# A decoder layer's feed-forward: gate and up by seven half-size products, their result through memory, then down in five slabs

## The chip, the cores and the metric

The kernel is one program on 1 core of a Trainium2 chip. The metric is the time of one execution on the device, in microseconds (us). TensorE, VectorE, ScalarE and GpSimd compute, SyncE issues the transfers; in the rows they are PE (PEld for its weight loads), DVE, ACT, POOL and SP.

## The reference

`x` has 4 sequences of 512 rows of 1024 numbers, 2048 rows in all, in float32. Self-attention and cross-attention come first and are not touched. What is changed is the last line:

```python
x = x + ffn(layernorm(x))
# Wg, Wu: 3584 x 1024, Wd: 1024 x 3584, each from 4-bit codes:
#   w = NF4_CODE[q];  w = w.reshape(-1, 64) * absmax[:, None]
g = x @ Wg.T
u = x @ Wu.T
h = silu(g) * u
y = h @ Wd.T
```

## The kernel before, in words

`attention` runs first and leaves its result `x2` in memory. `feed_forward` is a block of its own, each engine with its instruction list, joined by counting semaphores. An engine takes its list in order: a wait holds all that stands behind it.

**Numbers.** A float32 value `v` is cut into a float16 high part `v_h` (ScalarE) and the rest `v_l = v - v_h` (GpSimd, for the inputs VectorE), and a product is three matmuls: h·h, h·l, l·h.

**Weights.** The 3584 hidden columns are 28 chunks of 128. A chunk has a gate, an up and a down matrix of 128 x 1024, each made in two *tiles* of 128x512. For a tile SyncE loads `codes` (L1380) and `scales` (L1385), two tiles ahead. ScalarE draws eight straight lines of the codes (`draw_line`, L1547 and L1550), VectorE joins them by six maxima (L1625) and one difference (L1631), GpSimd multiplies by the scales (`scale`, L1426), ScalarE cuts the high part (L1555) and GpSimd the low (L1431). ScalarE's table of lines mixes the tiles: the high part of tile k is cut between lines of tile k+2.

**Input.** Sixteen rows of 128 of `x2` are kept in float32 in `y` (L1396). Each is normalised (statistics at L1639 to L1644, root on GpSimd at L1436, ScalarE at L1561), turned by TensorE (L1483) and cut (L1569, L1652), in part between the first matmuls.

**Products.** A group is two chunks; there are 14 groups. `gate_up` (L1501) makes for a chunk and a sequence the 128x512 gate and up, 24 matmuls each; ScalarE takes silu (L1578), VectorE multiplies (L1661), the result is cut into `hT_h` and `hT_l` (L1583, L1445). `down` (L1521) then makes for each of the 16 rows of 128 the group's share of the output, 12 matmuls, and VectorE adds it to `y` (L1666). So a group is 384 + 192 matmuls of 128x512, and the whole 14 x 576 = 8064. The group is a loop over one body, but for the first and the last. `out` is stored behind the last group's adds (L1404).

## Time and profile before

| | |
|---|---|
| median of 3 runs | 2796.19 us (2792.77 to 2798.71) |
| the profiled execution | 2796.21 us, its span 2794.3 us |
| busy: TensorE, VectorE, ScalarE, GpSimd | 92%, 74%, 56%, 44% of the span |
| feed-forward's first instruction | 950.7 us from the span's start |
| TensorE's share of the chain of waits | 60% (L1501 39%, L1521 21%) |

A matmul's recorded time overlaps with the next one's, so the pace is read from how many a stretch holds. A wait is put down to what came last.

### The profile page before, as it was taken

To read this page: it belongs to the slowest core of one execution; us is meant where nothing else is said; L and a number is where in the kernel's file an instruction comes from. 1 tells how busy PE (TensorE), PEld (TensorE's weight loads), DVE (VectorE), ACT (ScalarE), POOL (GpSimd) and SP (SyncE) were. 2 spreads that over 40 slices of the span, in tenths; PEclk is the share of its full clock that TensorE was granted. 3 is DMA by queue.
4 is the path that set the end of the run, shared out by engine and by line. 5 is a ranking of instruction groups with operands and counts; after the bars stand their busy time and mean duration, and the time that the engine had idled before them with its cause. 6 is when DMAs were issued, how large, how long until landed. Compare 5 with 4: busy or idle time off the path is not lost.

```text
span 2794.3 us, 52658 instructions
## 1 busy us (share of the span) xinstructions
PE 2581.9 (92%) x18536; PEld 1397.0 (50%) x18536; DVE 2054.9 (74%) x2844; ACT 1572.4 (56%) x2794; POOL 1235.5 (44%) x1068
## 2 busy tenths in 40 slices
PE   5889999999974359899999999999999999999999
PEld 3567767667663234344444444444444444444444
DVE  4656768767775768787787869788787868778773
ACT  3456666656663468474655647465564747465550
POOL 2356667767774424252433424243433425243330
PEclk9999999999987669999999999999999999999999
DMA  5243433333222321111111112121111212111112
GB/s 192 91 132 100 121 114 120 102 111 100 81 73 59 128 80 56 51 61 38 60 49 50 53 45 60 38 68 38 53 52 45 61 38 66 40 60 46 52 34 120
DMA packets 153268, 205.34 MB, mean 73 GB/s; under 512 B 34160, under 2 KB 85872, under 8 KB 153072
## 3 DMA queue, kind: packets, MB, share of 16 engines
q1 hardware_dynamic: 153072, 202.97, 23.0%
q8 instruction: 93, 1.52, 0.2%
q14 instruction: 103, 0.84, 0.1%
HBM read 157.16 MB, written 44.04 MB: 72 GB/s over the span
## 4 chain that ended last, share of the span: by engine, by line
PE 60%; DVE 2%; issue 1%; ACT 1%; DMA 1%; POOL 0%; SPq 0%; DVEq 0%; ACTq 0%; POOLq 0%
PE f_bank L1501 39%; PE f_down L1521 21%; DVE line L1625 1%; DMA codes<-in_codes 1%; DVE f_stats L1639 0%; DVE fT_l L1652 0%; ACT f_xn L1561 0%; ACT line L1550 0%; ACT fT_h L1569 0%; PE f_down L1483 0%; DVE w L1631 0%; ACT line L1547 0%; DVE h L1661 0%; DVE y L1666 0%; DVE f_mean_var L1642 0%
## 5 line engine op out<-in xcount | busy, mean ns | idle before, releaser
L1625 DVE TENSOR_TENSOR line<-line 128x512 f32<-128x512 f32 x1008 | 919.4, 962 | 46.7 <-issue 30.9
L1550 ACT ACTIVATE line<-codes 128x512 f32<-128x512 int32 x1008 | 591.2, 620 | 382.6 <-DVE line L1625 284.8
L1501 PE MATMUL f_bank<-fT_h,up_h 128*128 128x512 f16 x1792 | 680.2, 380 | 3.7 <-DVE fT_l L1652 2.4
L1501 PE MATMUL f_bank<-fT_l,up_h 128*128 128x512 f16 x1792 | 680.2, 380 | 0.0
L1501 PE MATMUL f_bank<-fT_h,up_l 128*128 128x512 f16 x1792 | 680.2, 380 | 0.0
L532 POOL TENSOR_TENSOR p_l<-p,p_h 128x512 f16<-128x512 f32 x320 | 369.9, 1164 | 243.0 <-ACT p_h L945 242.6
L1666 DVE SCALAR_TENSOR_TENSOR y<-f_down,y 128x1024 f32<-128x1024 f32 x224 | 274.2, 1224 | 190.7 <-PE f_down L1521 190.7
L1431 POOL TENSOR_TENSOR up_l<-w,up_h 128x512 f16<-128x512 f32 x112 | 145.8, 1301 | 529.2 <-ACT up_h L1555 529.2
L1426 POOL TENSOR_TENSOR w<-w,scales 128x512 f32<-128x512 f32 x168 | 263.8, 1570 | 227.7 <-DVE w L1631 227.7
L1115 DVE TENSOR_REDUCE block_max<-bank 128x4 f32<-128x512 f32 x320 | 218.8, 686 | 195.3 <-PE bank L704 193.0
L1521 PE MATMUL f_down<-dn_h,hT_h 128*128 128x512 f16 x896 | 340.6, 380 | 9.0 <-DVE y L1666 9.0
L937 ACT ACTIVATE p<-bank 128x512 f32<-128x512 f32 x320 | 190.9, 597 | 271.6 <-PE bank L733 269.7
L1521 PE MATMUL f_down<-dn_l,hT_h 128*128 128x512 f16 x896 | 340.6, 380 | 0.0
L1521 PE MATMUL f_down<-dn_h,hT_l 128*128 128x512 f16 x896 | 340.4, 380 | 0.0
L1501 PEld LDWEIGHTS f_bank<-fT_h,up_h 128*128 128x128 f16 x1792 | 175.5, 98 | 214.7 <-DVE fT_l L1652 2.8
L1501 PEld LDWEIGHTS f_bank<-fT_h,up_l 128*128 128x128 f16 x1792 | 175.5, 98 | 212.1 <-issue 1.1
L1501 PEld LDWEIGHTS f_bank<-fT_l,up_h 128*128 128x128 f16 x1792 | 175.5, 98 | 210.3 <-issue 0.6
L1445 POOL TENSOR_TENSOR hT_l<-h,hT_h 128x512 f16<-128x512 f32 x112 | 172.9, 1543 | 237.3 <-ACT hT_h L1583 237.3
L1547 ACT ACTIVATE line<-codes,above 128x512 f32<-128x512 int32 x168 | 119.9, 714 | 218.3 <-DVE line L1625 183.6
L674 PE MATMUL bank<-xT,w_h 128*128 128x512 f16 x720 | 220.2, 388 | 10.8 <-POOL vx_h L602 10.8
L1661 DVE SCALAR_TENSOR_TENSOR h<-f_bank,h 128x512 f32<-128x512 f32 x112 | 77.1, 688 | 164.5 <-PE f_bank L1501 156.6
L945 ACT ACTIVATE p_h<-p 128x512 f16<-128x512 f32 x320 | 192.0, 621 | 0.0
(157 smaller groups left out, 4245.4 us busy)
## 6 DMA issues: line engine op xcount, KB each, us to landing
codes<-in_codes SPq DMA_DIRECT2D x168, 256.0 KB, 3.0
scales<-in_scales SPq DMA_DIRECT2D x336, 128.0 KB, 2.9
nat_parts<-nat SPq DMA_DIRECT2D x48, 256.0 KB, 2.0
q_rows<-nat_parts SPq DMA_DIRECT2D x96, 128.0 KB, 2.7
x_unit<-in_x SPq DMA_DIRECT2D x64, 128.0 KB, 2.7
x<-x_unit SPq DMA_DIRECT2D x64, 128.0 KB, 2.3
y<-x SPq DMA_DIRECT2D x4, 2048.0 KB, 12.3
out<-y SPq DMA_DIRECT2D x16, 512.0 KB, 2.6
```

The lines of the kernel that those rows point to most:

```text
L532: nc.gpsimd.tensor_tensor(p_l[:, n % 2, k, :], p32[:, f % 3, :], p_h[:, n % 2, k, :], ALU.subtract).then_inc(p_low, 1)
L674: mm = nc.tensor.matmul(dst[:, :], w[:, c, cols], xT[:, :, half, c, :], start=(c == 0 and m == 0), stop=(c == CT - 1 and m == 2))
L937: nc.scalar.activation(p32[:, f % 3, :], bank[T_BANK + T_OF[f % CHUNKS]][:, :], ACT.Exp, scale=SELF_SCALE).then_inc(t_exp, 1)
L945: nc.scalar.activation(p_h[:, n % 2, k, :], p32[:, f % 3, :], ACT.Copy).then_inc(p_high, 1)
L1115: nc.vector.reduce_max(block_max[:, n % PAIRS, k, :], bank[S_BANK + S_OF[k]][:, :].rearrange("p (a n) -> p a n", n=P), AX_X)\
L1426: nc.gpsimd.tensor_tensor(w, w, scales[:, k % 2, :], ALU.mult).then_inc(scaled, 1)
L1445: nc.gpsimd.tensor_tensor(hT_l[:, q // NB, cols], h32[:, q % 2, :], hT_h[:, q // NB, cols], ALU.subtract).then_inc(h_low, 1)
L1501: mm = nc.tensor.matmul(bank[(GATE, UP)[kind] + n % 2][:, :], w[:, chunk, kind, P * c:P * c + P], x[:, c, cols], start=(m == 0), stop=(m = ...
L1521: mm = nc.tensor.matmul(down_bank[r % 2][:, half, :], h[:, m // 3, rows], w[:, m // 3, cols], start=(m == 0), stop=(m == 5))
L1550: op = nc.scalar.activation(line[:, m, :], codes[:, slot, :], ACT.Copy, scale=slope, bias=intercept)
L1625: nc.vector.tensor_tensor(line[:, n + 2, :], line[:, n, :], line[:, n + 2, :], ALU.max)\
L1666: nc.vector.scalar_tensor_tensor(y[:, r, :], down_bank[r % 2][:, :, :].rearrange("p a n -> p (a n)"), 1.0 / (H_SCALE * F_SCALE), y[:, r, : ...
```

## The change

`feed_forward` is written anew; nothing else is touched. 

**Phase 1, gate and up.** Take one matrix product for two chunks (256 columns), all 1024 inputs and two sequences; cut in halves along each side it is 2 x 2 blocks times 2 x 2 blocks. Instead of eight half-size products it makes seven, M1 to M7, of sums and differences of the blocks (Strassen's scheme), 12 matmuls each. The sums of the inputs are made once: the rows are taken in 8 *pairs* (row j and j + 8), turned, summed (`sums`), and kept as seven float16 pairs in `fx`. The sums of the weights are made per `k` (k even: gate of two chunks, odd: up; 28 values of k), from four *quarters* (tiles): GpSimd sums (`sum_w`), ScalarE and GpSimd cut, into one of two sides of `fw`. A *set* is the seven products for one k and one of two row halves (`nb`): 56 sets of 84 matmuls, 4704 in all. M4, M5 and M7 go on top of M2, M3 and M1 in PSUM, after ScalarE has copied M2 and M1 away and VectorE has taken a difference (`differ`); `join`, `left`, `right_sum` and `right` put the four result blocks together. Beside each set, in `half_step`, every engine makes two tiles of the next weights. The hidden values are stored to memory (`store_h`), 256 KB for each of 112 blocks.

**Tiles.** The six maxima are replaced by two `reduce_max`, each over four lines of 512 (2048 inputs, 512 outputs; the four numbers that it compares lie 2 KB apart).

**Phase 2, down.** `y` is loaded again, into space that the inputs had. The 28 chunks are five slabs of 3, 4, 7, 7 and 7. For each slab and each row of 128 the hidden values come back from memory (seven slots), 6 matmuls per chunk follow, and one add to `y`: 80 adds in place of 224. The tiles of a slab are made during the slab before, the first slab's in the last two half steps of phase 1 (three tiles in each). A row takes 18, 24 or 42 matmuls; phase 2 has 2688, as before.

The loop is gone: all is written out.

```diff
-y = sb("y", [P, RT, C], FP32)
-xT_h = sb("fT_h", [P, CT, B * T], FP16)
-xT_l = sb("fT_l", [P, CT, B * T], FP16)
+fx = sb("fx", [P, 2, 7, 2, KT * HALF], FP16)
+fw = sb("fw", [P, 2, 7, 2, HALF], FP16)
...
+PRODUCTS = (M2, M1, M3, M6, M4, M5, M7)
+POS = {m: n for n, m in enumerate(PRODUCTS)}
+PS_OF = {M1: 0, M2: 1, M3: 2, M6: 3, M4: 1, M5: 2, M7: 0}
+
+CUT = (M2, M4, M1, M3, M6, M5, M7)
+SUMMED = (M2, M1, M6, M5, M7)
+DIRECT = {M4: 1, M3: 2}
...
+SLABS = (3, 4, 7, 7, 7)
...
+    def store_h(n):
+        chunk, b, _ = h_at(n)
+        sp.wait_ge(h_low, n + 1)
+        sp.dma_start(dram["h"][QT * b:QT * b + QT, :, chunk, :].rearrange("q p n -> p q n"),
+                     h_box[:, n % BOXES, :, :, :].rearrange("p q a n -> p q (a n)"))\
+            .then_inc(box_stored[n % BOXES], 16)
...
+    for idx in range(3):
+        load_h(idx)
+    for h in range(8 * GROUPS - 4, 8 * GROUPS):
+        store_h(h)
+    sp.wait_ge(product, 7 * NSET)
+    for r in range(4):
+        sp.dma_start(y_row(r), dram["x2"][r // QT, P * (r % QT):P * (r % QT) + P, :]).then_inc(y_loaded[r], 16)
+    for idx in range(3, H_SLOTS):
+        load_h(idx)
+    sp.wait_ge(h_low, 8 * GROUPS)
+    for r in range(4, RT):
+        sp.dma_start(y_row(r), dram["x2"][r // QT, P * (r % QT):P * (r % QT) + P, :]).then_inc(y_loaded[r], 16)
+    for idx in range(NI):
+        for t in tiles_in(idx):
+            if t + 2 < LAST_TILE:
+                load_tile(t + 2)
+        if idx >= NI - RT:
+            r = idx - NI + RT
+            sp.wait_ge(y_added, idx + 1)
+            sp.dma_start(dram["out"][P * r:P * r + P, :], y_row(r)).then_inc(out_stored, 16)
+        if H_SLOTS <= idx + H_SLOTS - 1 < NI and idx >= 1:
+            load_h(idx + H_SLOTS - 1)
+    sp.wait_ge(out_stored, 16 * RT)
...
+    def pair(j):
+        for n in range(4):
+            x_cut_low(j, n)
+        if j + 2 < 8:
+            root(j + 2)
+        for n in range(4, 7):
+            x_cut_low(j, n)
...
+    def half_step(k, nb):
+        s = 2 * k + nb
+        tiles = tiles_of(k, nb)
+        last = s - 1
+        lows = [h_tile(last // 4, last % 2, c) for c in H_ORDER] if last >= 0 and last // 2 % 2 else []
+        for n in lows[0:2]:
+            hidden_low(n)
+        if nb == 1 and k + 1 < NK:
+            cut_low(k + 1, M2)
+            cut_low(k + 1, M4)
+        scale(tiles[0])
+        if nb == 0 and k >= 0:
+            cut_low(k, M5)
+            cut_low(k, M7)
+        if nb == 1 and k + 1 < NK:
+            sum_w(k + 1, M1)
+        if k >= 0:
+            join(s)
+        if nb == 1 and k + 1 < NK:
+            sum_w(k + 1, M6)
+        for n in lows[2:4]:
+            hidden_low(n)
+        if nb == 1 and k + 1 < NK:
+            cut_low(k + 1, M1)
+            cut_low(k + 1, M3)
+        scale(tiles[1])
+        if nb == 0 and k + 1 < NK:
+            sum_w(k + 1, M2)
+        if nb == 1 and k + 1 < NK:
+            sum_w(k + 1, M5)
+            cut_low(k + 1, M6)
+            sum_w(k + 1, M7)
...
-    def gate_up(i, chunk, first=False):
-        for nb in range(NB):
-            n = NB * chunk + nb
-            cols = slice(T * nb, T * nb + T)
-            if first:
-                pe.wait_ge(ln_low, 8 * (nb + 1))
-            for kind in range(2):
-                if nb == 0:
-                    pe.wait_ge(w_low, PER * i + 4 * chunk + 2 * kind + 2)
-                if n >= 2:
-                    pe.wait_ge((silu_done, h_done)[kind], NQ * i + n - 1)
-                for m in range(3 * CT):
-                    c = m // 3
-                    w, x = ((up_h, xT_h), (up_h, xT_l), (up_l, xT_h))[m % 3]
-                    mm = nc.tensor.matmul(bank[(GATE, UP)[kind] + n % 2][:, :],
-                                          w[:, chunk, kind, P * c:P * c + P], x[:, c, cols],
-                                          start=(m == 0), stop=(m == 3 * CT - 1))
-                    if m == 3 * CT - 1:
-                        mm.then_inc((gate_done, up_done)[kind], 1)
-                    if first and nb < NB - 1 and kind == 0 and m % 6 == 5:
-                        ln_turn(4 * (nb + 1) + m // 6)
+    def multiply(s, m):
+        k, nb = s // 2, s % 2
+        pe.wait_ge(w_low, 7 * k + CUT_AT[m] + 1)
+        if m == M4:
+            pe.wait_ge(copied, 2 * s + 1)
+        if m == M5:
+            pe.wait_ge(differed, s + 1)
+        if m == M7:
+            pe.wait_ge(copied, 2 * s + 2)
+        out = ps[:, 4 * (s % 2) + PS_OF[m], :]
+        for n in range(3 * KT):
+            c = n // 3
+            w, x = ((0, 0), (0, 1), (1, 0))[n % 3]
+            mm = nc.tensor.matmul(out, fw[:, k % 2, m, w, P * c:P * c + P],
+                                  fx[:, nb, m, x, HALF * c:HALF * c + HALF],
+                                  start=(n == 0 and m in (M1, M2, M3, M6)),
+                                  stop=(n == 3 * KT - 1), skip_group_check=m in (M4, M5, M7))
+        mm.then_inc(product, 1)
+
+    def product_set(s):
+        if s < 2:
+            pe.wait_ge(x_low, 28 * (s + 1))
+        else:
+            pe.wait_ge(right_done, s - 1)
+        for n, m in enumerate(PRODUCTS):
+            multiply(s, m)
+            if s == 0 and n in (0, 1, 3):
+                turn((5, 6, None, 7)[n])
...
+    def half_step(k, nb):
+        s = 2 * k + nb
+        tiles = tiles_of(k, nb)
+        last = s - 1
+        highs = [h_tile(last // 4, last % 2, c) for c in H_ORDER] if last >= 0 and last // 2 % 2 else []
+        draw(tiles[0], 0)
+        if k >= 0:
+            copy(s, 0)
+        if last >= 0 and last // 2 % 2 == 0:
+            silu(last, C22)
+            silu(last, C11)
+        for n in highs[0:2]:
+            hidden_high(n)
+        if nb == 1 and k + 1 < NK:
+            cut_high(k + 1, M2)
+            cut_high(k + 1, M4)
+        draw(tiles[0], 1)
+        if k >= 0:
+            copy(s, 1)
+        for n in highs[2:4]:
+            hidden_high(n)
+        if nb == 0 and k >= 0:
+            cut_high(k, M5)
+            cut_high(k, M7)
+        draw(tiles[1], 0)
+        if nb == 1 and k + 1 < NK:
+            cut_high(k + 1, M1)
+            cut_high(k + 1, M3)
+        draw(tiles[1], 1)
+        if nb == 1 and k + 1 < NK:
+            cut_high(k + 1, M6)
...
+    for idx in range(NI):
+        for t in tiles_in(idx):
+            draw(t, 0)
+            draw(t, 1)
+            down_high(t)
...
-    def look_up(i, ops):
-        for at in ops:
-            k, n = at // LUT, at % LUT
-            t = AHEAD + PER * i + k
-            if n < LUT - 1:
-                dve.wait_ge(lined, NL * t + n + 3)
-                if n >= 2:
-                    dve.wait_ge(lut, LUT * t + n - 1)
-                nc.vector.tensor_tensor(line[:, n + 2, :], line[:, n, :], line[:, n + 2, :], ALU.max)\
-                    .then_inc(lut, 1)
-            else:
-                dve.wait_ge(lut, LUT * t + n)
-                if k >= 2 - AHEAD:
-                    dve.wait_ge(w_low, t - 1)
-                nc.vector.tensor_tensor(w32[:, k % 2, :], line[:, NL - 2, :], line[:, NL - 1, :], ALU.subtract)\
-                    .then_inc(lut, 1)
+    def reduce(t, which):
+        dve.wait_ge(lined, 8 * t + 4 * which + 4)
+        if t >= 1:
+            dve.wait_ge(lut, LUT * t)
+        nc.vector.reduce_max(side[:, which, :], line[:, which, :, :].rearrange("p m n -> p n m"), AX_X)\
+            .then_inc(lut, 1)
...
+    def half_step(k, nb):
+        s = 2 * k + nb
+        up = k % 2
+        tiles = tiles_of(k, nb)
+        if s >= 1:
+            finish(s - 1)
+        look_up(tiles[0])
+        if k >= 0:
+            differ(s)
+        reduce(tiles[1], 0)
+        if k >= 0:
+            left(s)
+            if up:
+                dve.wait_ge(left_done, s + 1)
+                times_gate(s, C22, c32[:, 0, :])
+        reduce(tiles[1], 1)
+        subtract(tiles[1])
+        if k + 1 == NK:
+            look_up(tiles[2])
+        if k >= 0:
+            for n, c in enumerate((C21, C12)):
+                if up:
+                    dve.wait_ge(product, 7 * s + POS[(M4, M5)[n]] + 1)
+                    times_gate(s, c, bank(s, 1 + n))
+                right_sum(s, n)
...
+    for j in range(8):
+        sums(j)
+        if j + 2 < 8:
+            stat(j + 2)
+            normal(j + 2)
+        if j == 0:
+            half_step(-1, 0)
+        if j == 2:
+            half_step(-1, 1)
+    for k in range(NK):
+        for nb in range(2):
+            half_step(k, nb)
+    finish(NSET - 1)
+    for idx in range(NI):
+        for t in tiles_in(idx):
+            look_up(t)
+        add_down(idx)
```

ScalarE in the last group before: lines (L1547, L1550), `h` from the banks (L1578) and high cuts (L1555) are mixed.

```order
L1547 ACTIVATE line<-codes,above 128x512 [waits lut,codes_loaded0]
L1547 ACTIVATE line<-codes,below 128x512 [waits lut]
L1550 ACTIVATE line<-codes 128x512 [waits lut]
L1555 ACTIVATE up_h<-w 128x512 [waits scaled]
L1550 ACTIVATE line<-codes 128x512 [waits lut]
L1583 ACTIVATE hT_h<-h 128x512 [waits h_done]
L1550 ACTIVATE line<-codes 128x512 [waits lut] x4
L1547 ACTIVATE line<-codes,above 128x512 [waits lut,codes_loaded1]
```

And ScalarE in phase 2 of the change (`fx` is where the down weights lie there, L1765 is `down_high`, L1738 and L1741 are `draw`):

```order
L1738 ACTIVATE line<-codes,above 128x512 [waits lut,codes_loaded1]
L1741 ACTIVATE line<-codes 128x512 x3
L1738 ACTIVATE line<-codes,below 128x512 [waits lut]
L1741 ACTIVATE line<-codes 128x512 x3
L1765 ACTIVATE fx<-quarter 128x512 [waits product,scaled]
L1738 ACTIVATE line<-codes,above 128x512 [waits lut,codes_loaded0]
```

The high cut of a tile now stands between its own lines and the next tile's, and waits for that tile's scaling.

GpSimd at the half step of even k and nb = 0 (L1582 `hidden_low`, L1553 `scale`, L1569 `cut_low` of M5 and M7, L1588 `join`):

```order
L1582 TENSOR_TENSOR h_box<-h,h_box 128x4x128 [waits h_high] x2
L1553 TENSOR_TENSOR quarter<-quarter,scales 128x512 [waits lut,scales_loaded0]
L1569 TENSOR_TENSOR fw<-w_sum,fw 128x512 [waits fw_high] x2
L1588 TENSOR_TENSOR c<-c 128x512 [waits differed,copied]
L1582 TENSOR_TENSOR h_box<-h,h_box 128x4x128 [waits h_high] x2
L1553 TENSOR_TENSOR quarter<-quarter,scales 128x512 [waits lut,scales_loaded1]
```

`scale` of the next chunk's first tile, which needs both of its reduces, stands ahead of the low cuts of M5 and M7, which TensorE waits for in the same set.

## Rows read from the trace of the kernel before

**Rows 1.** The page: busy us (share of the span) x instructions, by engine
```profile
PE 2581.9 (92%) x18536; PEld 1397.0 (50%) x18536; DVE 2054.9 (74%) x2844; ACT 1572.4 (56%) x2794; POOL 1235.5 (44%) x1068
```
**Rows 2.** The chain of waits in order of time: start us, us, what
```profile
1173.85 82.88 PE f_bank L1501 x384
...
2748.57 41.45 PE f_down L1521 x192
2790.05 1.23 DVE y L1666
```
**Rows 3.** Windows: us, busy (x) of PE, PEld, DVE, ACT, POOL, clock, DMA share, GB/s
```profile
1346.00:2600.00 1254.00, 1254.00 (x5812) 568.49 (x5811) 991.68 (x1090) 715.81 (x1254) 474.41 (x325) 1.00 0.16 51
955.40:1050.00 94.60, 42.92 (x197) 25.05 (x198) 67.97 (x124) 62.07 (x106) 27.31 (x54) 0.66 0.35 122
969.50:990.00 20.50, 0.00 (x0) 0.00 (x0) 15.05 (x25) 6.88 (x14) 5.88 (x4) 0.50 0.99 366
```
**Rows 4.** Groups by line: xcount | busy us, mean ns | idle before
```profile
L1625 DVE TENSOR_TENSOR line<-line 128x512 f32<-128x512 f32 x1008 | 919.4, 962 | 46.7 <-issue 30.9 <-ACT line L1550 11.5 <-ACT line L1547 4.3
L1666 DVE SCALAR_TENSOR_TENSOR y<-f_down,y 128x1024 f32<-128x1024 f32 x224 | 274.2, 1224 | 190.7 <-PE f_down L1521 190.7
L1115 DVE TENSOR_REDUCE block_max<-bank 128x4 f32<-128x512 f32 x320 | 218.8, 686 | 195.3 <-PE bank L704 193.0
L1067 DVE TENSOR_SCALAR xn<-xn,mean_var,rstd 128x1024 f32<-128x1024 f32 x14 | 11.3, 806 | 1.6 <-POOL rstd L526 1.6
L1661 DVE SCALAR_TENSOR_TENSOR h<-f_bank,h 128x512 f32<-128x512 f32 x112 | 77.1, 688 | 164.5 <-PE f_bank L1501 156.6 <-ACT h L1578 7.1
```
**Rows 5.** Timeline, ScalarE at one tile: start us, us, instruction [idle before]
```profile
989.89 0.72 ACT L1547 ACTIVATE line<-codes,above 128x512 f32<-128x512 int32 x1 [13.62 <-DMA codes<-in_codes]
990.52 0.70 ACT L1547 ACTIVATE line<-codes,below 128x512 f32<-128x512 int32 x1
991.13 3.21 ACT L1550 ACTIVATE line<-codes 128x512 f32<-128x512 int32 x6
994.25 0.61 ACT L1555 ACTIVATE up_h<-w 128x512 f16<-128x512 f32 x1
```
**Rows 6.** Timeline, ScalarE's passes back to back in the steady part
```profile
1701.14 0.58 ACT L1578 ACTIVATE h<-f_bank 128x512 f32<-128x512 f32 x1
1701.62 0.62 ACT L1550 ACTIVATE line<-codes 128x512 f32<-128x512 int32 x1
```
**Rows 7.** GpSimd by line: duration ns min/median/max, first and last start
```profile
L1426 POOL TENSOR_TENSOR w<-w,scales x168: 1257/1711/1724, 960.6 to 2713.8; 128x512 f32<-128x512 f32 x168
...
L1431 POOL TENSOR_TENSOR up_l<-w,up_h x112: 1151/1314/1622, 963.6 to 2686.5; 128x512 f16<-128x512 f32 x112
```
**Rows 8.** Timeline, hand-over from VectorE to GpSimd
```profile
966.14 0.69 DVE L1631 TENSOR_TENSOR w<-line 128x512 f32<-128x512 f32 x1
...
967.01 1.26 POOL L1426 TENSOR_TENSOR w<-w,scales 128x512 f32<-128x512 f32 x1 [2.06 <-DVE w L1631]
```
**Rows 9.** Timeline, the pieces of a layernorm row
```profile
979.86 1.28 DVE L1639 BATCH_NORM_STATS2 f_stats<-y 128x6 f32<-128x512 f32 x2
981.18 0.21 DVE L1642 BATCH_NORM_AGGREGATE f_mean_var<-f_stats 128x2 f32<-128x12 f32 x1
...
996.14 0.55 POOL L1436 TENSOR_TENSOR f_rstd<-f_var_eps,f_minus_half 128x1 f32<-128x1 f32 x1
...
998.11 1.94 PE L1483 MATMUL f_down<-f_ident,f_xn 128*128 128x128 f32 x8 [52.06 <-ACT f_xn L1561]
```
**Rows 10.** Timeline, SyncE's issues at the start and of y
```profile
950.94 0.34 SPq L1380 DMA_DIRECT2D codes<-in_codes  x1
...
969.52 1.68 SPq L1396 DMA_DIRECT2D y<-x  x3
...
971.31 3.26 SPq L1380 DMA_DIRECT2D codes<-in_codes  x1
```

763 lines of the change are left out of this document (464 added, 299 removed).

## The prediction

> **What bounds the kernel now.** I read the page first: TensorE is busy 92% of the span, VectorE 74% [rows 1]. A mean over stages says little, so next the chain of waits: from 1173.85 us on it is TensorE alone, 384 matmuls in 82.88 us and 192 in 41.45 us, up to one last add [rows 2]. That is 0.2158 us per matmul, no gap, and the clock of that stretch is 1.00, TensorE's upper level of 2.4 GHz [rows 3]. Feed-forward's 8064 matmuls at that pace are 1740.3 us. They end at 2790.0, so TensorE works as if it had started at 1049.7 without a stop; the block's first load is issued at 950.94 [rows 10], so its start costs 98.8 us. VectorE is busy 992 of 1254 us in the steady part, ScalarE 716 [rows 3]: they are hidden, with 21% and 43% to spare.
>
> **What is taken away.** 5376 gate and up matmuls become 4704: 672 x 0.2158 = **145.0 us**. Down keeps 2688, 580.1 us. A set of 84 takes 18.13 us, a product of 12 takes 2.59. All else is whether the other engines still hide.
>
> **Prices.** ScalarE: the eight lines of a tile take 4.45 us, so one side of four 2.25 [rows 5]; other passes follow each other at 0.48 to 0.55, I take 0.5 [rows 6]. VectorE: a pass of 512 is 0.69 long and one of 1024 is 1.22 [rows 4], so 0.54 per 512 numbers and 0.15 fixed, and two stand 0.60 apart [rows 9]. GpSimd: 1.26 for scaling and 1.15 for a cut at the shortest [rows 7], and 0.18 from VectorE's end to its start [rows 8]. For the new `reduce_max` of 2048 numbers there is no row. Its nearest is the reduce of 512 at 0.686, whose numbers lie side by side [rows 4]. At the same rate it is 4 x 0.536 + 0.15 = 2.30 us; at the upper end, with two steps for each number since they lie 2 KB apart, 4.44. I take 2.30, as no strided operation in these rows is seen to be slower.
>
> **The start, +33.** A pair of rows needs on GpSimd seven low cuts and a root (8.6 us), but not in one piece. The root of pair j+2 stands in the middle of pair j and waits for statistics that VectorE takes only behind pair j's five sums. There are three slots for sums, so the fourth waits for the third low cut. By the pieces of rows 9: about 4.7 us to the last sum, 3.3 for the statistics of two rows, 0.75 for the root, three cuts 3.5, so 12.5 to 13 us a pair for six pairs and 8.7 for two. The normalising pass is 0.81 per row [rows 4] and lies beside the cuts. The first pair begins some 16 us in. Two half steps of tiles lie between (10 and 14 us). The first set starts some 93 us after the first load, and three turns of 3.9 us (16 transposes, [rows 9]) lie between its products. It then stops at M4: that waits for ScalarE's copy, which waits for all eight pairs' cuts, at about 138. M5 waits until 144.5, the second set starts at 149.7. Less one set, this is a start at 131.6 in place of 98.8. Bounds: 10 if the roots don't hold GpSimd, 45 if the engines hinder each other.
>
> **Phase 1, +62.** In four sets (72.5 us) VectorE has 16 reduces, 8 subtractions, 20 passes on the banks and 8 products: 58 us. ScalarE has some 55, GpSimd 51. None is full, but each list is in order and the chain goes round all three. From the start of a second set of odd k (0): M2 is done at 2.8, ScalarE copies, cuts two results and two weights, draws the lower side of tile 1 (7.65); reduce and subtraction (10.7), scaling and one sum (13.2), cuts of M1 and M3 (14.3), the lower side of tile 2 (16.6), reduce and subtraction (19.9), two products and two sums (22.3), the last block and its product (24.0), the next set's copy and two cuts (25.6), lower side (27.9), reduce and subtraction (30.9), scaling (32.4), and only then the low cut of M5 (33.5). TensorE wants it at 18.1 + 5 x 2.59 = 31.1: 2.4 us late. Walked on, the fourth set's last product comes 2.4 us after the point at which this round began with its copy, so the round itself is that much longer: 4.8 us per four sets, 13 rounds, 62 us. Bounds: 14 with one microsecond a round, 91 with seven.
>
> VectorE's maxima take 0.96 in the mean and its plain passes on a bank 0.69 [rows 4], and GpSimd's scaling 1.71 in the median against 1.26 at the shortest [rows 7]: here the two hinder each other. By the Trainium skill (SBUF — State Buffer, section "SBUF: two separate sides") a VectorE operation with two SBUF inputs and a GpSimd one exclude each other, and a reduce with one input would not; then the shortest times are right, and with the medians instead the sum would be some 17 us longer.
>
> **Phase 2, +82.** The last two half steps make three tiles each, with high cuts that wait for scalings: by the same walk row 0 ends 11 us late. Then 9.2 MB of `y` and hidden values are asked for before the codes of the ninth tile. Before, 7.5 MB went in 20.5 us [rows 3], and ScalarE stood 13.6 us for codes that were issued behind three loads of `y` [rows 5, 10]. So those codes come about 25 us after the loads, and they start only when the last hidden values are cut, 17 us after the nominal end of phase 1.
>
> From there a loop binds. ScalarE's list is draw, draw, high cut, and the cut waits for the tile's own scaling. A tile takes 4.45 + 0.05 + 2.30 + 0.72 + 0.18 + 1.26 + 0.1 + 0.5 = **9.6 us**. Slab 1 has 16 rows x 24 x 0.2158 = 82.9 us of matmuls and must see 14 tiles: 134 us. Slab 0 (62.2 us) ends with its sixth tile after the codes, at 43 + 58 = 101 us. In slabs 2 and 3 a row is 9.06 us and 14 tiles fit into 16 rows (134 against 145). They and slab 4 go at TensorE's pace, 3 x 145.0 less 7.8 of their first row that is done while it waits: 427. Together 101 + 134 + 427 = 662 against 580. VectorE's adds (80 in place of 224, at 1.22) lie in the gaps. Bounds: 60 to 100.
>
> **Sum.** -145.0 + 33 + 62 + 82 = +32. The sum stands against the profiled execution's 2796.2 us, which is the median (2796.19) too: **2828 us**.
>
> **The rivals.**
> *The lists of phase 1 run far enough apart* (faster). If the low cut of M5 and the copy of the next round come before TensorE wants them, phase 1 costs nothing: -145 + 33 + 82 = -30, 2766 us. It decides at 2.4 us in a chain of 33, so at 7% of it: ScalarE's spare 43% and hand-overs shorter than I count speak for it, the medians in rows 7 against.
>
> *Each number of the strided reduce costs two steps* (far slower). At 4.44 us VectorE has 16 x 4.36 + 23 = 93 us in four sets against 72.5: +281 over 14 rounds. A tile in phase 2 takes 2.25 + 8.9 + 2.7 = 13.9: 43 + 48 tiles x 13.9 + 145 - 8 = 847, +267. The start takes 17 more. -145 + 33 + 281 + 17 + 267: about 3250 us. Rows 4 show a reduce at full rate, but on numbers side by side, so they neither bear it out nor exclude it. The Trainium skill (Advanced Engine Details and Errata, "SBUF Cachelines") says that a 16-byte line wants two hits to hide its latency, and here each access is on another line; no row of before shows that penalty.
>
> *The change gives less than its 672 matmuls*, if the products on top of others don't go back to back. The matmuls have the same shape and the same two operands' places as before, so I give it nothing of its own.
>
> **Chances.** The forecast (three places bind, 2787 to 2900) has 0.50; the fast rival 0.30, from 2725 with a cheap start to 2785; the strided reduce 0.17; 0.03 is left for an end above 2925 for other reasons or below 2725. The range is 2725 to 2925; it leaves out the strided reduce and that rest. Of the forecast case 0.01 is faster and 0.05 within 0.2%, which is about what a measurement of this kernel can tell from no change. So faster 0.31, same 0.05, slower 0.64. The likeliest case's own range is 2787 to 2900.
>
> **What would show it.** In the profile after: 4704 + 2688 matmuls of 512 columns; TensorE's idle time before M5 on GpSimd's low cut, some 5 us in every four sets; in slabs 0 and 1 TensorE waiting for down weights at 9.6 us per tile, and none in slabs 2 to 4; ScalarE's idle time before its high cut, 4.4 us per tile; the reduce at 2.3 us. A reduce near 4.4 makes the forecast wrong by hundreds; phase 1 in 1015 us makes it wrong by 62; a first set not held at M4 by 20 or more.

## The result: 3178.6 us, and the profile after

The changed kernel takes **3178.55 us** (median of 4 runs, 3176.19 to 3182.88) against 2795.79 before (4 runs on the same chip): ratio 1.1371, interval 1.1354 to 1.1388. The forecast was 2828, its range 2725 to 2925; the rival that priced the strided reduce at two steps per number had about 3250. The profiled execution took 3180.82 us, its span is 3179.0.

The page of the changed kernel: busy us by engine, and the shares of the chain that ended last.
```profile
PE 2564.3 (81%) x17864; PEld 1356.6 (43%) x17864; DVE 2427.2 (76%) x2332; ACT 1635.4 (51%) x2998; POOL 1519.0 (48%) x1363
...
DVE 18%; PE 16%; issue 9%; ACT 8%; POOL 5%; DMA 1%; SPq 0%; DVEq 0%; POOLq 0%; ACTq 0%
```
The 672 matmuls are gone (18536 [rows 1] to 17864), and still the kernel is 383 us longer. The chain of before was TensorE alone from 1173.85 us on [rows 2]; now VectorE, ScalarE and GpSimd hold more of it than TensorE. VectorE has 512 instructions fewer than before and is busy for 372 us more. Its groups, and the two others that matter (xcount | busy us, mean ns of one | idle before, ended by):
```profile
L1916 DVE TENSOR_REDUCE side<-line 128x512 f32<-128x2048 f32 x336 | 1247.7, 3727 | 209.4 <-ACT line L1741 208.8
L1682 PE MATMUL f_ps<-fx,fw 128*128 128x512 f16 x4704 | 1103.4, 398 | 197.1 <-POOL fw L1569 152.1
...
L1553 POOL TENSOR_TENSOR quarter<-quarter,scales 128x512 f32<-128x512 f32 x168 | 213.6, 1272 | 968.5 <-DVE quarter L1928 968.5
```
One reduce takes 3.73 us, not 2.30. The work that it replaces, three maxima of 0.96 [rows 4], took 2.9. The 4704 matmuls of phase 1 are all there.

The trace by stage: sets 2 to 56 of phase 1 (from the 85th of its 4704 matmuls on), then phase 2 (length, busy us and instructions of PE, PEld, DVE, ACT, POOL, granted clock, DMA share, GB/s).
```profile
1130.20:2386.40 1256.20, 1076.91 (x4621) 461.84 (x4619) 1151.14 (x716) 761.61 (x1410) 726.06 (x601) 0.93 0.23 70
2386.40:3174.70 788.30, 620.23 (x2688) 269.99 (x2688) 503.48 (x240) 254.38 (x460) 132.12 (x109) 0.89 0.29 93
```
In the steady part of before, TensorE had no gap at a clock of 1.00 and VectorE was busy 79% of the time [rows 3]. In phase 1 now VectorE is busy 92%, TensorE stands idle for 179 us, and its 4620 matmuls take 80 us more than 0.2158 each. So a stop costs twice, once as idle time and once in the clock behind it.

One round of four sets in phase 1, TensorE's timeline (start us, us, instruction, [idle before]):
```profile
1668.17 34.06 PE L1682 MATMUL f_ps<-fx,fw 128*128 128x512 f16 x144 [6.09 <-POOL fw L1569]
1702.92 5.35 PE L1682 MATMUL f_ps<-fx,fw 128*128 128x512 f16 x24 [0.68 <-POOL fw L1569]
1712.13 19.63 PE L1682 MATMUL f_ps<-fx,fw 128*128 128x512 f16 x84 [3.86 <-POOL fw L1569]
1734.36 19.98 PE L1682 MATMUL f_ps<-fx,fw 128*128 128x512 f16 x84 [2.60 <-DVE c L1936]
1759.70 30.53 PE L1682 MATMUL f_ps<-fx,fw 128*128 128x512 f16 x133 [5.37 <-POOL fw L1569]
```
The round is 91.5 us in place of 72.5: 12.5 of idle time (0.68, 3.86, 2.60, 5.37) and 6.5 of slower matmuls. The mean of the 13 rounds is 90.9.

One tile of phase 2, ScalarE, VectorE and GpSimd:
```profile
2611.77 0.71 ACT L1738 ACTIVATE line<-codes,below 128x512 f32<-128x512 int32 x1
2611.89 7.25 DVE L1916 TENSOR_REDUCE side<-line 128x512 f32<-128x2048 f32 x2 [3.15 <-ACT line L1741]
...
2619.18 0.69 DVE L1928 TENSOR_TENSOR quarter<-side 128x512 f32<-128x512 f32 x1
...
2620.02 1.26 POOL L1553 TENSOR_TENSOR quarter<-quarter,scales 128x512 f32<-128x512 f32 x1 [9.09 <-DVE quarter L1928]
...
2621.31 0.63 ACT L1765 ACTIVATE fx<-quarter 128x512 f16<-128x512 f32 x1 [7.28 <-POOL quarter L1553]
...
2621.85 0.70 ACT L1738 ACTIVATE line<-codes,above 128x512 f32<-128x512 int32 x1
```
This is the loop that the prediction walked: draw, draw, reduce, subtract, scale, high cut, draw. Its period is 12.3 us, not 9.6. With a reduce of 2.30 the first one hides behind the drawing of the lower side, with 3.73 both lie on the path (7.25 in one piece). Fourteen tiles at 12.3 are 172 us, so now slabs 2 and 3 are bound too: TensorE's last waits for a slab's weights end at 2684.5, 2859.9 and 3035.3, 175 us apart in place of 145. Only what follows goes at TensorE's pace.

Where the miss lies, by stage. The right column is experiment e_pairs, in which the reduce takes 2.28 us:

| us | forecast | changed kernel | reduce at 2.28 |
|---|---|---|---|
| second set starts at | 1100.6 | 1130.2 | 1114.6 |
| sets 2 to 56 | 1059.0 | 1256.2 | 1109.8 |
| phase 2 | 662.0 | 788.3 | 670.9 |

The forecast's column is its own sum: 950.94 + 149.7, then 55 sets at TensorE's pace (997.0) + 62, then 580 + 82. The columns differ by 30 + 197 + 126 = 353 us (the whole miss), and by 14 + 51 + 9 = 74 where the reduce has its forecast price.

### The profile page after: what moved, and what is told of

It reads as the page before. It is cut to its first block, busy times and chain, and to the rows that moved or that the text cites. A ratio compares the mean times of both kernels' runs of the same rounds, so it can differ in the third digit from the quotient of the medians.

```text
span 3179.0 us, 47439 instructions
## 1 busy us (share of the span) xinstructions
PE 2564.3 (81%) x17864; PEld 1356.6 (43%) x17864; DVE 2427.2 (76%) x2332; ACT 1635.4 (51%) x2998; POOL 1519.0 (48%) x1363
## 4 chain that ended last, share of the span: by engine, by line
DVE 18%; PE 16%; issue 9%; ACT 8%; POOL 5%; DMA 1%; SPq 0%; DVEq 0%; POOLq 0%; ACTq 0%
DVE side L1916 13%; PE f_ps L1682 11%; PE f_ps L1714 5%; ACT line L1741 4%; POOL quarter L1553 3%; DVE quarter L1928 2%; ACT line L1738 2%; POOL fw L1569 1%; DVE h L1942 1%; DVE c L1972 1%; ACT h_box L1813 1%; ACT fw L1753 1%; DMA codes<-in_codes 1%; DVE c L1961 0%; POOL c L1588 0%
## 5 line engine op out<-in xcount | busy, mean ns | idle before, releaser
L1916 DVE TENSOR_REDUCE side<-line 128x512 f32<-128x2048 f32 x336 | 1247.7, 3727 | 209.4 <-ACT line L1741 208.8
L1682 PE MATMUL f_ps<-fx,fw 128*128 128x512 f16 x4704 | 1103.4, 398 | 197.1 <-POOL fw L1569 152.1
L1682 PEld LDWEIGHTS f_ps<-fx,fw 128*128 128x128 f16 x4704 | 471.7, 102 | 827.4 <-POOL fw L1569 183.0
L1553 POOL TENSOR_TENSOR quarter<-quarter,scales 128x512 f32<-128x512 f32 x168 | 213.6, 1272 | 968.5 <-DVE quarter L1928 968.5
L1741 ACT ACTIVATE line<-codes 128x512 f32<-128x512 int32 x1008 | 556.0, 615 | 0.0
L1714 PE MATMUL f_ps<-fx,fw 128*128 128x512 f16 x1188 | 279.3, 398 | 84.1 <-POOL fx L1576 54.5
L1714 PE MATMUL f_ps<-fx 128*128 128x512 f16 x924 | 211.2, 390 | 52.6 <-POOL fx L1576 43.3
L1714 PEld LDWEIGHTS f_ps<-fx,fw 128*128 128x128 f16 x1188 | 119.9, 102 | 241.1 <-POOL fx L1576 57.6
L1765 ACT ACTIVATE fx<-quarter 128x512 f16<-128x512 f32 x44 | 27.7, 630 | 333.5 <-POOL quarter L1553 333.5
L1561 POOL TENSOR_TENSOR w_sum<-quarter 128x512 f32<-128x512 f32 x140 | 181.8, 1299 | 10.6
L1569 POOL TENSOR_TENSOR fw<-w_sum,fw 128x512 f16<-128x512 f32 x140 | 161.1, 1159 | 31.7 <-ACT fw L1753 31.7
L697 PE MATMUL bank<-k_rows,q_rows 96*128 96x512 f16 (+3 forms) x512 | 136.8, 306 | 18.7 <-DMA q_rows<-nat_parts 12.3
L1582 POOL TENSOR_TENSOR h_box<-h,h_box 128x512 f16<-128x512 f32 x112 | 134.1, 1217 | 36.4 <-ACT h_box L1813 35.8
L726 PE MATMUL bank<-q_rows,k_rows 97*128 97x512 f16 (+3 forms) x512 | 136.6, 305 | 14.5 <-DVE px_l L1149 10.4
```

Of the source, the lines that this page charges most:

```text
L1553: nc.gpsimd.tensor_tensor(w, w, scales[:, t % 2, :], ALU.mult).then_inc(scaled, 1)
L1561: nc.gpsimd.tensor_tensor(w_sum[:, SUM_SLOT[m], :], quarter[:, a, :], quarter[:, b, :], op)\
L1569: nc.gpsimd.tensor_tensor(fw[:, k % 2, m, 1, :], w_source(m), fw[:, k % 2, m, 0, :], ALU.subtract)\
L1682: mm = nc.tensor.matmul(out, fw[:, k % 2, m, w, P * c:P * c + P], fx[:, nb, m, x, HALF * c:HALF * c + HALF], start=(n == 0 and m in (M1, M ...
L1714: mm = nc.tensor.matmul(ps[:, 2 * (idx % 4) + half, :], hT[:, n, h, :], d[:, w, HALF * half:HALF * half + HALF], start=(n == 0 and m == 0) ...
L1741: op = nc.scalar.activation(out, codes[:, t % 2, :], ACT.Copy, scale=slope, bias=intercept)
```

## The experiments

Each kernel starts from the changed one, and each ratio is to the kernel before on the same chip; over the chips used the kernel before takes 2795.6 to 2798.0 us, so a difference between two experiments on different chips is good to some 2 us. The edits are shown without their semaphores. Two theories stand first. **A**: the reduce is slow since the four numbers of each output lie 2 KB apart. **B**: it is slow since each output takes only four numbers (short runs), or the loops around VectorE would stop TensorE at any price of it.

### a_maxima: three maxima in place of the reduce

```diff
-nc.vector.reduce_max(side[:, which, :], line[:, which, :, :].rearrange("p m n -> p n m"), AX_X)
+for m in (0, 2):
+    nc.vector.tensor_tensor(line[:, which, m, :], line[:, which, m, :], line[:, which, m + 1, :], ALU.max)
+nc.vector.tensor_tensor(side[:, which, :], line[:, which, 0, :], line[:, which, 2, :], ALU.max)
```


> Of the changed kernel, only the price of a side is changed: three maxima of 512 in place of the reduce over four lines that lie 2 KB apart (3.73 us in its profile). Theory 1, the reduce is the step that was mis-sized and the rest of the forecast's sum holds: a side costs 1.9 to 2.3 us (three passes 0.6 to 0.72 apart), the tile loop of phase 2 falls from 12.3 to 9.3 to 9.6 us, the round of four sets of phase 1 from 91.3 to 74 to 80 us, and the time is 2800 to 2870. Theory 2, the loops round the engines are what costs and the reduce only lies in them: rounds stay above 85 us and the time above 2950. If the maxima and GpSimd hinder each other as before the change (0.96 a maximum), the rounds lie at 80 to 84 and the time at 2860 to 2930.

Measured: 3018.14 us, ratio 1.0793 (1.0775 to 1.0811), 160 us less than with the reduce. Groups of VectorE and GpSimd in this kernel:
```profile
L1918 DVE TENSOR_TENSOR line<-line 128x512 f32<-128x512 f32 x672 | 677.5, 1048 | 174.6 <-ACT line L1742 172.6
L1921 DVE TENSOR_TENSOR side<-line 128x512 f32<-128x512 f32 x336 | 323.3, 962 | 11.6
```
```profile
L1570 POOL TENSOR_TENSOR fw<-w_sum,fw 128x512 f16<-128x512 f32 x140 | 192.5, 1383 | 25.5 <-ACT fw L1754 25.5
...
L1589 POOL TENSOR_TENSOR c<-c 128x512 f32<-128x512 f32 x56 | 96.0, 1714 | 0.0
```
A side takes 2.98 us (1001 us over 336), so it is cheaper than the reduce of 3.73. In the changed kernel the same two GpSimd operations take 1.16 and 1.27. Beside maxima GpSimd grows slower, beside reduces it does not: what VectorE gains here GpSimd gives back in part, and the round in phase 1 is 89.3 us, hardly shorter. In a round VectorE's busy time falls only from 83.2 to 79.5 us and GpSimd's rises from 53.2 to 62.8. No run shows by itself that GpSimd's rise is what keeps the round long. Phase 2 gains: a tile takes 9.2 us, and the last three slabs run as one stretch of 429.07 us (forecast 427). Time and round are those of theory 2 in the expectation, but a side came out at 2.98 us and not at 1.9 to 2.3, so this run doesn't yet tell the price from the loops.

### b_side_by_side: the four numbers next to each other

```diff
-line = sb("line", [P, 2, 4, HALF], FP32)
+line = sb("line", [P, 2, HALF, 4], FP32)
...
-out = line[:, which, m, :]
+out = line[:, which, :, m]
...
-nc.vector.reduce_max(side[:, which, :], line[:, which, :, :].rearrange("p m n -> p n m"), AX_X)
+nc.vector.reduce_max(side[:, which, :], line[:, which, :, :], AX_X)
```


> The lines are laid out so that the four numbers that a reduce compares lie side by side; ScalarE writes each line at every fourth place. Theory 1 (the distance of the reads costs): the reduce falls to 2.3 us and the time to 2800 to 2880, if ScalarE's writes cost no more. Rival (each output of only four inputs costs an extra, whatever the place): the reduce stays at 3.7 and the time at 3178. If ScalarE's writes 16 bytes apart become slow in their turn, its passes are over 0.62 and the gain is in part gone.

Measured: 3191.71 us, ratio 1.1419 (1.1399 to 1.1439). Groups of VectorE and of ScalarE:
```profile
L1916 DVE TENSOR_REDUCE side<-line 128x512 f32<-128x2048 f32 x336 | 767.3, 2284 | 687.7 <-ACT line L1741 687.5
```
```profile
L1741 ACT ACTIVATE line<-codes 128x512 f32<-128x512 int32 x1008 | 1008.5, 1144 | 0.0
```
The reduce of the same 2048 numbers falls to 2.28 us, the forecast's own price, with runs as short as ever: theory A. But ScalarE now writes at a distance of 16 B and takes 1.14 per line where it took 0.615, so the penalty has moved to the writer. It costs as much there, since ScalarE stands in both loops. It is the last case of the expectation, with nothing left of the gain.

### c_draw_ahead: ScalarE draws the next tile before it waits

```diff
-for idx in range(NI):
-    for t in tiles_in(idx):
-        draw(t, 0)
-        draw(t, 1)
-        down_high(t)
+late = [t for idx in range(NI) for t in tiles_in(idx)]
+for n, t in enumerate(late):
+    draw(t, 0)
+    draw(t, 1)
+    if n >= 1:
+        down_high(late[n - 1])
+down_high(late[-1])
```


> Only ScalarE's order in phase 2 is changed: it draws tile t+1 before it cuts the high part of tile t; the reduce is left. Theory (a serial loop draw, reduce, scale, cut of 12.3 us per tile binds phase 2): the period falls to what VectorE needs, two reduces, a subtraction and its adds, 9 to 9.5 us, and slabs 2 and 3 come to TensorE's 145 us: 100 to 120 us less, 3060 to 3080. Rival (VectorE or the transfers are the bound of phase 2 anyway): less than 30 us.

Measured: 3067.37 us, ratio 1.0969 (1.0950 to 1.0988), 111 us less, with the reduce as slow as before. ScalarE in phase 2:
```profile
2804.32 0.72 ACT L1738 ACTIVATE line<-codes,above 128x512 f32<-128x512 int32 x1 [2.75 <-DVE side L1918]
...
2810.10 0.61 ACT L1765 ACTIVATE fx<-quarter 128x512 f16<-128x512 f32 x1
2813.46 0.72 ACT L1738 ACTIVATE line<-codes,above 128x512 f32<-128x512 int32 x1 [2.75 <-DVE side L1918]
```
The high cut waits for a scaling 3 times (23 us), where it waited 52 times (396 us), and the period is 9.14 us, set by VectorE, which is busy for 9.11 of it. So phase 2 was bound by the order of one list, as forecast. The reduce's price entered through it, and in part through VectorE itself: with this order phase 2 takes 678 us here and 616 with the reduce at 2.28 (g_pairs_draw_ahead).

### d_probes: the price by distance

At the end of the changed kernel, behind its last use of `line`, VectorE makes single operations on it, twice over, and ScalarE writes copies into it.
```diff
+for b in (1, 2, 4, 8, 16, 128, 512):
+    tick(nc.vector.reduce_max(side[:, 0, :].rearrange("p (a b) -> p a b", b=b),
+                              flat(0).rearrange("p (a m b) -> p a b m", m=4, b=b), AX_X))
+tick(nc.vector.reduce_max(side[:, 0, 0:32], flat(0).rearrange("p (n m) -> p n m", m=64), AX_X))
+tick(nc.vector.reduce_max(side[:, 0, 0:32], flat(0).rearrange("p (m n) -> p n m", n=32), AX_X))
...
```


> The changed kernel with a row of single operations behind its end, each waiting for the one before; some 60 to 70 us longer. On VectorE the same reduce of 2048 float32 numbers to 512 with its four inputs 4, 8, 16, 32, 64, 512 and 2048 bytes apart, and to 32 outputs of 64 inputs each, near and far; a maximum of two 512-number operands in line and at distances of 1 KB, 512 B, 256 B and 16 B; on ScalarE a copy written in line and at every fourth place. Theory 1: the time follows the distance (2.3 us at 4 and 8 bytes, 3.7 from 16 bytes on, also with 64 inputs per output). Rival: 3.7 at every distance with four inputs, 2.3 with 64 inputs.

Measured (one execution, 3245.92 us). VectorE's timeline, four numbers per output at 4, 8, 16, 32, 64, 512 and 2048 B from each other, then 64 numbers per output at 4 B and at 128 B:
```profile
3174.64 2.29 DVE L2070 TENSOR_REDUCE side<-line 128x512 f32<-128x2048 f32 x1 [2.84 <-ACT line L1885]
3176.96 2.29 DVE L2070 TENSOR_REDUCE side<-line 128x512 f32<-128x2048 f32 x1
3179.28 3.77 DVE L2070 TENSOR_REDUCE side<-line 128x512 f32<-128x2048 f32 x1
3183.09 3.78 DVE L2070 TENSOR_REDUCE side<-line 128x512 f32<-128x2048 f32 x1
3186.91 3.57 DVE L2070 TENSOR_REDUCE side<-line 128x512 f32<-128x2048 f32 x1
...
3194.16 3.62 DVE L2070 TENSOR_REDUCE side<-line 128x512 f32<-128x2048 f32 x1
3197.82 2.29 DVE L2072 TENSOR_REDUCE side<-line 128x32 f32<-128x2048 f32 x1
3200.14 3.57 DVE L2073 TENSOR_REDUCE side<-line 128x32 f32<-128x2048 f32 x1
```
The step lies between 8 and 16 B, and beyond it distance changes little. With 64 numbers per output the two prices are the same 2.29 and 3.57: short runs cost nothing, and B's first half falls. Two-input maxima of 512 are dearer too once operands and output are out of line (0.69 in line, 1.07 to 1.25 at 16 to 1024 B; nothing between was tried), and so are ScalarE's copies (0.63 in line, about 1.1 written at every fourth place).

### e_pairs: pairs of neighbours

A layout with 8 B between the numbers of an output, and in which ScalarE writes two neighbours at a time:
```diff
-line = sb("line", [P, 2, 4, HALF], FP32)
+line = sb("line", [P, 2, HALF // 2, 4, 2], FP32)
...
-out = line[:, which, m, :]
+out = line[:, which, :, m, :]
+code = codes[:, t % 2, :].rearrange("p (a b) -> p a b", b=2)
...
-nc.vector.reduce_max(side[:, which, :], line[:, which, :, :].rearrange("p m n -> p n m"), AX_X)
+nc.vector.reduce_max(side[:, which, :].rearrange("p (a b) -> p a b", b=2),
+                     line[:, which, :, :, :].rearrange("p a m b -> p a b m"), AX_X)
```


> The changed kernel with its lines laid out so that the four numbers of a reduce lie 8 bytes apart, at which the probe took 2.29 us (3.6 to 3.8 from 16 bytes on); ScalarE writes a line as pairs of neighbours, 32 bytes from pair to pair. This is the reduce at the price of the forecast. Theory 1 (the forecast's sum holds but for that price): ScalarE's passes stay at 0.62, the tile loop of phase 2 is 9.2 to 9.6 us, a round of four sets in phase 1 75 to 80 us, the time 2815 to 2880. Theory 2 (phase 1's loop was undercounted too, as the run with maxima suggests with rounds of 89 us at 2.98 us a side): rounds of 82 to 87 us and 2890 to 2960. Rival: pairs don't spare ScalarE, passes of 0.9 to 1.1 and no gain, 3100 or more.

Measured: 2902.41 us, ratio 1.0386 (1.0368 to 1.0403): **276 us** less than the changed kernel, by the layout of one buffer. Groups of VectorE and ScalarE:
```profile
L1917 DVE TENSOR_REDUCE side<-line 128x512 f32<-128x2048 f32 x336 | 765.2, 2283 | 315.3 <-ACT line L1742 314.9
```
```profile
L1742 ACT ACTIVATE line<-codes 128x512 f32<-128x512 int32 x1008 | 585.0, 653 | 0.0
```
The reduce has the forecast's price and ScalarE pays 0.04 per line. This is the kernel that the prediction described, so it measures the rest of it: still 74 us above the forecast and 107 above before. That is the time of the expectation's theory 2, with a round (79.6, in the mean of 13 rounds 80.5) near that of theory 1. TensorE in a round of phase 1 and up to the next, and two windows behind the stop that ends at 1670.47:
```profile
1590.89 36.43 PE L1682 MATMUL f_ps<-fx,fw 128*128 128x512 f16 x168 [3.22 <-POOL fw L1569]
1628.32 18.30 PE L1682 MATMUL f_ps<-fx,fw 128*128 128x512 f16 x84 [1.00 <-POOL fw L1569]
1647.81 7.93 PE L1682 MATMUL f_ps<-fx,fw 128*128 128x512 f16 x36 [1.19 <-DVE c L1938]
...
1670.47 38.12 PE L1682 MATMUL f_ps<-fx,fw 128*128 128x512 f16 x168 [3.22 <-POOL fw L1569]
```
```profile
1671.07:1674.47 3.40, 3.40 (x10) 1.21 (x8) 3.40 (x3) 2.39 (x5) 3.40 (x4) 0.50 0.15 53
1674.48:1690.00 15.52, 15.52 (x73) 7.06 (x72) 11.07 (x10) 10.60 (x19) 7.01 (x7) 1.00 0.28 85
```
The stop that recurs is the one forecast, before M5 on GpSimd's low cut. The round is 79.6 us: 6.2 of it idle (two waits of 0.4 lie in the lines left out). The same 168 matmuls take 36.43 us behind the one stop and 38.12 behind the other, since the granted clock is at its lower level (0.50, 1.2 GHz) for 3.4 us there, from 0.6 us after the first matmul on. That costs 1.7 us. Of the 13 such stops (twelve of 3.2 us, one of 4.8) 8 are followed by such a stretch and 5 are not.

### f_pairs_cut_first: GpSimd cuts M5 and M7 before it scales

```diff
-scale(tiles[0])
 if nb == 0 and k >= 0:
     cut_low(k, M5)
     cut_low(k, M7)
+scale(tiles[0])
```


> As e_pairs, and GpSimd cuts the low parts of M5 and M7 before it scales the next weights' first tile (even k, first half). Theory (the stall of 2.5 to 5 us before M5 in the first half of every k is that place in GpSimd's list): these stalls go, 28 times; the round falls by 4 to 8 us and the time by 40 to 100 against e_pairs. Rival (VectorE's list is the bound and TensorE waits for the next thing at once): under 15 us.

Measured: 2869.62 us, ratio 1.0259 (1.0242 to 1.0276), 33 less than e_pairs: a little under the expectation. The stop before M5 shrinks from 3.22 to 1.96 us and stays. So the cut's place behind the scaling is one link of the loop, not all of it. The clock takes back some of the gain: 12 of the 13 shorter stops are followed by 3.4 us at the lower level, where it was 8 of 13.

### g_pairs_draw_ahead: e_pairs with c's order

> As e_pairs, and ScalarE draws the next tile before it cuts a tile's high part in phase 2. Theory: slab 1 falls from 129 to 134 us to near TensorE's 83 to 95, slab 0 by some 15, so 45 to 65 us less than e_pairs. Rival (transfers or VectorE hold phase 2 then): under 20 us.

Measured: 2845.81 us, ratio 1.0179 (1.0162 to 1.0196), 57 less than e_pairs, as expected. With the reduce at 2.28 the order of phase 2 is worth half of what it was worth with 3.73 (111).

### h_all_four: e, f and g, and the late loads of y one per stretch

```diff
-for r in range(4, RT):
-    sp.dma_start(y_row(r), ...)
 for idx in range(NI):
     for t in tiles_in(idx):
         if t + 2 < LAST_TILE:
             load_tile(t + 2)
+    for r in range(4 + idx, min(5 + idx, RT)):
+        sp.dma_start(y_row(r), ...)
```


> All of these together, and in addition the last twelve loads of y are issued one row at a time between the loads of codes. Theory: the codes of the ninth tile come 12 to 16 us earlier, so the sum of f's and g's gains plus some 10 us: 90 to 150 us less than e_pairs, 2720 to 2790, at or below the time before the change. Rival: what is freed in one place is taken by the next wait, and it ends above 2830.

Measured: 2806.41 us, ratio 1.0041 (1.0025 to 1.0057). That is 96 less than e_pairs, where f and g alone give 33 and 57: the edits add up, and at most some 6 us are left for the loads. The 96 lie in the expected 90 to 150, and the time lies 16 above the 2720 to 2790 given with them; 2902 less 90 to 150 is 2752 to 2812.

### i_root_last: GpSimd takes the root behind all seven cuts of its pair

```diff
-for n in range(4):
-    x_cut_low(j, n)
-if j + 2 < 8:
-    root(j + 2)
-for n in range(4, 7):
-    x_cut_low(j, n)
+for n in range(7):
+    x_cut_low(j, n)
+if j + 2 < 8:
+    root(j + 2)
```


> As h_all_four, and GpSimd takes the root for pair j+2 behind pair j's seven low cuts and not between them. Theory of the start (GpSimd stands at the root for statistics while three cuts wait, some 3 us in each of six pairs): the second set starts 12 to 25 us earlier and the time falls by as much. Rival (VectorE's statistics and sums are the bound of the start): under 5 us.

Measured on top of h_all_four: 2796.79 us (11 runs), ratio 0.9999 (0.9990 to 1.0008), 9.6 less. M5 of the first set starts at 1098.14 in place of 1109.74. Two roots that follow each other on GpSimd in e_pairs, with the root still in the middle:
```profile
1050.51 0.70 POOL L1531 TENSOR_TENSOR f_rstd<-f_var_eps,f_minus_half 128x2 f32<-128x2 f32 x1 [4.15 <-DVE f_var_eps L1890]
...
1064.06 0.69 POOL L1531 TENSOR_TENSOR f_rstd<-f_var_eps,f_minus_half 128x2 f32<-128x2 f32 x1 [4.15 <-DVE f_var_eps L1890]
```
A pair takes 13.5 us there and 11.7 here. The root in the middle of a pair does hold GpSimd, as forecast, though for less than I expected of this run.

### j_draw_both: ScalarE draws both sides of a tile before it copies

```diff
 draw(tiles[0], 0)
+draw(tiles[0], 1)
 if k >= 0:
     copy(s, 0)
...
     cut_high(k + 1, M4)
-draw(tiles[0], 1)
 if k >= 0:
     copy(s, 1)
```


> As h_all_four, and ScalarE draws both sides of a half step's first tile before it copies M2, so that it draws while it would wait for VectorE to free the copy's place. Theory of phase 1's loop (the lower side comes 3 to 4 us late, since it stands behind that copy): the first subtraction comes 2 us earlier in each set, the round of four sets falls from 77 to 73.5 to 75.5 us and the time by 20 to 45. Rival (VectorE's own list or the copy itself binds): under 8 us, or slower, if the copy comes later and M4 waits.

Measured on top of h_all_four: 2731.23 us, ratio 0.9763 (0.9750 to 0.9776): 75 less, far more than expected. TensorE's timeline in the middle of phase 1:
```profile
1499.83 220.44 PE L1683 MATMUL f_ps<-fx,fw 128*128 128x512 f16 x1020
```
No stop at all, and 0.2161 us per matmul. ScalarE's wait for VectorE before its copies tells why (us in total, times, longest), in h_all_four:
```profile
ACT c L1796 <- DVE h L1947: 139.3, 26, 6.2
```
In j_draw_both it is 34.5 us, and VectorE's wait for ScalarE's lines falls with it, from 196 to 121. In all of sets 2 to 56 TensorE is idle for 1.7 us, in h_all_four for 54.8. Before the edit ScalarE stood at this copy with a tile's lower side undrawn behind it; VectorE then had nothing to reduce, was late with the adds that free the next copy, and so ran the loop. With both sides drawn first VectorE has work while ScalarE waits. The prediction had this loop in its walk, but took only its end, GpSimd's cut, for what to cut.

### k_all_six: h, i and j together

> Both of these on top of h_all_four. Theory: the gains add, as start and rounds are apart: 30 to 70 us under h_all_four's 2806, 2735 to 2775, so faster than the kernel before the change by 1 to 2%. Rival: they don't add, 2790 or more.

Measured: **2717.53 us** (5 runs, 2715.88 to 2720.57), ratio 0.9715 (0.9702 to 0.9729): 80 us faster than the kernel before on its chip and 461 than the changed one, with the same number of instructions on each engine. The gains add, and the time is below the expected 2735 to 2775, since j's gain was above its own expectation. Its steady part, its start, and the end of phase 1:
```profile
1500.00:2000.00 500.00, 500.00 (x2318) 226.51 (x2316) 423.99 (x358) 393.19 (x705) 379.33 (x306) 1.00 0.29 88
```
```profile
1090.94 39.26 PE L1681 MATMUL f_ps<-fx,fw 128*128 128x512 f16 x169 [11.55 <-ACT c L1794]
...
2110.17 1.27 POOL L1552 TENSOR_TENSOR quarter<-quarter,scales 128x512 f32<-128x512 f32 x1 [2.92 <-DVE quarter L1931]
...
2112.75 1.40 SPq L1475 DMA_DIRECT2D fx<-h_parts  x3
...
2115.96 13.94 PE L1713 MATMUL f_ps<-fw,fx 128*128 128x512 f16 x54 [15.38 <-issue]
```
TensorE is at its pace with VectorE busy 85%, ScalarE 79% and GpSimd 76%: the stages now bound are the start and the first 180 us of phase 2. Against before: -145 for the matmuls; the second set starts at 1101.3, which is a start 33.5 longer; sets 2 to 56 take 2.2 more than 997.0; the last product ends at 2100.6 and the last matmul at 2709.7, 29.1 more than 580.1. Together -80.2, and so the spans differ.

The 15.4 us at the start of phase 2 have no releaser in the view, but the lines above order them. TensorE wants the hidden values of row 0. Their load is issued at 2112.75, behind a load of scales that waits in SyncE's list for a scaling of GpSimd, which ends at 2111.44. The last piece of row 0 lands at 2115.87, and the first matmul starts at 2115.96. In e_pairs the same three times are 2230.84, 2234.96 and 2235.05.

### l_strided_rest: k_all_six with the reduce of the change

> As k_all_six, but with the reduce as in the change, its four numbers 2 KB apart at 3.6 to 3.8 us. Theory (with the lists in order, VectorE's own work is what is left of the reduce's price): four sets need 16 x 3.65 + 23 = 81 us of VectorE against 72.5, so rounds of 81 to 83 us, some 125 us more in phase 1, 40 to 60 in slabs 0 and 1, 10 in the start: 2880 to 2920. Rival (the loop round the engines, and not the load, made the reduce cost what it did): rounds near 75 us and under 2820.

Measured: 2987.96 us, ratio 1.0679 (1.0655 to 1.0703), above the expected range. VectorE in phase 1:
```profile
1500.00:2000.00 500.00, 441.94 (x1946) 192.81 (x1945) 484.28 (x302) 324.14 (x591) 310.38 (x256) 0.96 0.25 74
```
VectorE is 97% busy and the round is 86.3 us. With the order mended it is VectorE's load that binds: the strided reads cost 270 us with the lists in the better order and 276 in the given one. Of the second half of B only this much is left: the loops in the given order stop TensorE at a reduce of 2.28 too, which is most of the 74 us of e_pairs, but they don't make the price of the strided reduce. The miss in my expectation lies in phase 1, 194 us longer than in k_all_six where I had 125: a round holds 83.7 us of VectorE's work, not 81, and VectorE is idle for 2.7 of it.

## Why the prediction was wrong, point by point

**Prices: the step that failed.** It put the new reduce at 2.30 us, at the rate of a reduce whose numbers lie side by side [rows 4], "as no strided operation in these rows is seen to be slower". But these rows hold no reduce over distant numbers, so they had no say. It takes 3.73: less the 0.15 fixed, 1.67 times the forecast's rate, between one step per number and the two of the upper end (4.44). At the measured price the three stages give 276 us more (e_pairs against the changed kernel), of a miss of 350. The changed kernel thus went by the rival *Each number of the strided reduce costs two steps*: its places and its order of size are right (a tile of 13.9 us, measured 12.3), its price is too high by a fifth, and the range left it out. The rule named there (the Trainium skill, Advanced Engine Details and Errata, "SBUF Cachelines") has runs d_probes and e_pairs on its side: two numbers in a 16-byte line (8 B apart) go at full rate, single ones from 16 B on do not. The measured factor was 1.6 in time.

**672 matmuls, -145: right.** In k_all_six and j_draw_both phase 1 runs at 0.216 per matmul, so the third rival (products on top of others not back to back) is out.

**The start, +33: too small by 14** with the reduce at its forecast price. Most of this stands before the first product: it starts at 1055.5 in e_pairs, and the walk had 93 us after the first load, 1044. GpSimd's list shows where. A pair with a root in its middle takes 13.5 us and not 12.5 to 13, six times, and the two half steps of tiles between the pairs take 12.1 and 18.6 us and not 10 and 14. The root itself was counted: it costs 11.6 in all (i_root_last), and with it mended the start is still 33.5 to 35.5 longer than before. The stop at M4 for ScalarE's copy came, but for 8.7 us only: 9.0 and 5.1 of the 23 that the walk had there stand before two of the turns.

**Phase 1, +62: the loop right, its size not.** e_pairs has 113 us above 0.2158 per matmul where the sum had 62. Idle time is 86 (6.2 in the round shown, forecast 4.8). The other 27 are 15 of slower matmuls (nine stretches of 3.4 us at the lower clock) and 12 of restarts behind some 67 stops, since the record of a matmul lasts 0.38 us where the pace is 0.216. The sum left them out though [rows 3] show clocks of 0.50 and 0.66 where TensorE pauses. The loads were nearly right: VectorE, ScalarE and GpSimd are busy for 60.4, 56.7 and 53.8 us of a round (forecast 58, 55 and 51). What closed the loop was found only by j_draw_both. It is also the answer to the rival *The lists of phase 1 run far enough apart*, which I gave 0.30: in the given order they don't, in another they do, and the load never was the bound at 2.28 us.

**Phase 2, +82: right in kind and nearly in size.** By stage 662 were forecast, 671 measured in e_pairs; from the last wait for weights on, 427 against 429, and a tile 9.6 against 9.7. The loop goes through the high cut as written (c_draw_ahead, g_pairs_draw_ahead take it away). The codes behind `y` landed 24 us after the first of its twelve late loads, and 43.9 us after the end of phase 1 (forecast 25 and 43).

**GpSimd beside VectorE: right.** Beside one-input reduces its scaling takes 1.27, the shortest of [rows 7], and beside two-input maxima its join takes 1.71 (a_maxima), the median there. In k_all_six, which has no maxima, 25 of the 68 low cuts of a quarter still take over 1.3 us, and each of the 25 overlaps VectorE's difference of two sides, an operation with two inputs. That is what the rule of the Trainium skill (SBUF — State Buffer, "SBUF: two separate sides") says.
